# A two-layer graph network on one core: exchanged operands in the degree products, and 16-bit three-part rows in the first layer's gathered sums

## The chip, the cores and the metric

One core of a Trainium2 chip runs the whole program. The metric is device time in microseconds (us) of one execution. TensorE (PE) multiplies matrices and has a separate record for each weight load (PEld); VectorE (DVE), ScalarE (ACT) and GpSimd (POOL) work on tiles; SyncE (SP) issues the plain DMAs and POOL the gathers.

## The reference, cut to what matters

There are 12,500 nodes of 32 features and 212,500 edges sorted by destination. The first layer sums, for every destination, the source rows weighted by the degrees of both ends, adds x and normalises. The second layer computes messages with a small network per edge, sums them the same way and normalises again.

```python
deg = segment_sum(ones, col)
deg_inv_sqrt = where(deg > 0, rsqrt(maximum(deg, 1.0)), 0.0)
norm = deg_inv_sqrt[row] * deg_inv_sqrt[col]
out = segment_sum(x[row] * norm[:, None], col)
x = layernorm(x + out)
x = layernorm(x + L1(x, edge_index, edge_attr_4, edge_attr_32, W1, b1, W2, b2, si_w0, si_w1))
```

## The kernel before, in words

Edges lie in tiles of 128 (one edge per partition), 16 tiles to a chunk. 1664 tiles are needed. An output node's sum is made by TensorE: gathered source rows are the weights of a matmul and a one-hot matrix of the destinations is the moving operand, so the sums land transposed in PSUM and DVE adds them into `sumT_all`, whose columns are nodes.

**Setup.** DVE builds one-hot matrices and TensorE counts the degrees with products (line 721): for each of 11 offsets (`TWIN`) DVE writes a weighted one-hot `ahi` (two operations, lines 1089 and 1092, two buffers in turn) and TensorE runs 16 products. There the shifted one-hot `lox` (128 contiguous 16-bit columns) is the weight and `a[0:CHUNKS, :, t]` (98 columns, each 16 elements from the next) is the moving operand. After the loop DVE remaps gather indices (lines 1114 and 1116; POOL finishes them, 546 and 548), makes the keys of the counted tiles (lines 1118 to 1130), and then, once the degrees are there, the inverse roots and the scaled table of x (lines 1131 to 1146). SP writes that table to memory (463); POOL waits for it and gathers.

**First layer.** It treats its tiles in two ways at once. 880 tiles go through 80 units of 11 tiles: DVE makes two one-hots for a tile (`spread_tile`, 1322 and 1324), TensorE makes a 128-partition count of source rows from them in three products (`count_tile`, 813) into one of two PSUM rings, ACT (10 of 11 tiles, line 619) or DVE (one, line 1331) copies the counts to SBUF, and one unit later TensorE multiplies the counts with the table in SBUF (`apply_counts`, 828: 98 products of 96 columns for a unit). The table holds each scaled row as three 16-bit parts (high, middle, low: ACT lines 605 and 609, DVE lines 1312 and 1316), so its sums have 96 rows and the parts are joined later by a product with `parts` (line 800).

The other 784 tiles are 49 chunks that are gathered. POOL issues 16 indirect DMAs for a chunk (line 551), each fetching 128 rows of 32 fp32 numbers (128 B) from the scaled table, into one of two buffers `xg`. DVE writes the fp32 one-hots of a chunk (`one_hots`, 1190), TensorE makes the sums (`window_sums`, 753: 16 fp32 products of 32 weight and 76 moving columns, each recorded as two), and DVE adds them (`add_gathered`, 1367).

The order is written out by hand. `turn(u)` fixes on TensorE, for every unit, where the sums of a chunk stand (after the count of tile 7 in the units that `chunk_turn` names, 49 of the 80), and POOL may start a quarter of a chunk only when TensorE has reached a pacing point (`s_pace`) and the buffer is free (`s_sum`). The engines run their lists in order: while TensorE waits for a chunk's rows, the units wait too.

**Second layer.** It starts when the first is normalised: POOL gathers normalised rows from `x1_table`, DVE forms products and reductions for each edge (lines 1498, 1504 and 1514). All values take the branch `all_near == 1`; the other branch (`wide_sums`, `add_wide_sums`) doesn't run.

Of the kernel before, what the change touches and what calls it, by code (L numbers as in the profile page):

```python
# [9 lines left out]
I32 = mybir.dt.int32  # L10
# [41 lines left out]
def gnn_program(nc, x_d, src_d, dst_d, first_d, efT_d, sh_d, w1_d, b1_d, w2_d, si_d, out_d):  # L52
# [96 lines left out]
    with ctx:  # L149
# [8 lines left out]
        x1_d = nc.dram_tensor("x1_table", (NPAD, D), F32).ap()  # L158

# [58 lines left out]
        xg = [sb(f"xg{k}", [P, TPC, D]) for k in range(2)]  # L218
# [4 lines left out]
        oh_all = [sb(f"oh{k}", [P, TPC, SW]) for k in range(2)]  # L223
        oh = [[o[:] for o in oh_all]] * 2
        idx0_block = oh_all[1][:].rearrange("p t w -> p (t w)")[:, 0:CG * TPC].bitcast(I32)
# [27 lines left out]
        high = oh_all[0][:].rearrange("p t w -> p (t w)")[:, 0:DT]  # L253
# [5 lines left out]
        ident_b = sb("ident_b", [P, P], BF16)  # L259
# [9 lines left out]
        tile_at = z_row[0:U].rearrange("p g f -> p (g f)")[:, 2 * P + 32:2 * P + 32 + UT]  # L269
        unit_rise = z_sq[:].rearrange("p g f -> p (g f)")[:, 3 * P - 32:3 * P - 32 + U]  # L270
        blocks = q_sb[:, 0:NP, :]
        picked = flat1[:, 0:HB * D].rearrange("p (h f) -> p h f", f=D)
        part_rows = flat1[:, 512:512 + HBS * D].rearrange("p (j f) -> p j f", f=D)
# [18 lines left out]
        ps_sum = [ps[0:m, 7 - l, 0:SPC * SW].rearrange("p (s w) -> p s w", s=SPC) for l, m in enumerate((D, DM))]  # L292
        ps_rows = [ps[:, 7, 0:GB * D]] * 2
# [7 lines left out]
        ps_deg = ps[:, 7, 0:NP]  # L301
        ps_count = ps[0:CHUNKS, 6, 0:TPC * TWIN]
# [19 lines left out]
        s_degree = sem("s_degree")  # L322
        s_root = sem("s_root")
# [3 lines left out]
        s_own = sem("s_own")  # L327
        s_remap = sem("s_remap")
# [82 lines left out]
        def _(sp):  # L411
# [59 lines left out]

            for k in range(2):
                sp.wait_ge(s_g[k], 16 * TPC * ((CG + 1 - k) // 2))
# [29 lines left out]
        def _(pool):  # L503
# [193 lines left out]
        def _(pe):  # L697
# [157 lines left out]
            def pick_rows(tile):  # L855
                pe.wait_ge(s_ohs, tile * 2 + 3)
                pe.matmul(ps_low, ohlow[:, 0, 0:P], ident_b[:], start=True, stop=True).then_inc(s_turned, 1)
# [13 lines left out]
            with pe.Else():  # L871
# [15 lines left out]
                with pe.Fori(1, CG // 2) as i:  # L887
                    for k in range(2):
                        wide_sums(0, xg[k], 2 * i + k, (s_g[k], 16 * TPC * i + 16 * TPC))
                wide_sums(0, xg[0], CG - 1, (s_g[0], 16 * TPC * (CG // 2) + 16 * TPC))  # L890
# [89 lines left out]
        def _(dve):  # L980
# [79 lines left out]
            with dve.If(all_near == 1):  # L1060
# [23 lines left out]
                for i in range(TWIN):  # L1084
                    if i >= 2:
# [8 lines left out]
                                      ALU.mult).then_inc(s_ndoh, 1)  # L1094
            with dve.Else():
# [22 lines left out]
            dve.memset(var[:], 1.0).then_inc(s_key, 1)  # L1118
            dve.wait_ge(s_src, 16 * SRC_LOADS)
            dve.tensor_scalar(low[:].bitcast(I32), dsrc, P - 1, None, ALU.bitwise_and).then_inc(s_key, 1)  # L1120
            dve.tensor_scalar(key[:].bitcast(I32), dsrc, 7, None, ALU.logical_shift_right).then_inc(s_key, 1)
            dve.wait_ge(s_key, 2)
            dve.tensor_copy(low[:], low[:].bitcast(I32)).then_inc(s_key, 1)
            dve.wait_ge(s_key, 3)
            dve.tensor_copy(high, key[:].bitcast(I32)).then_inc(s_key, 1)
            dve.wait_ge(s_key, 5)
            for to, of, offset in zip(counted_places(key), counted_places(high), counted_tiles(rel_tile)):
                dve.scalar_tensor_tensor(out=to, in0=of, scalar=float(TWIN), in1=offset, op0=ALU.mult,
                                         op1=ALU.add).then_inc(s_key, 1)

# [17 lines left out]
            dve.memset(eps[:], EPS).then_inc(s_w2x, 1)  # L1148

# [34 lines left out]
            def one_hots(layer, n):  # L1184
# [5 lines left out]
                dve.tensor_tensor(oh[layer][k], rel_b[:, a:a + TPC].unsqueeze(2).to_broadcast([P, TPC, SW]),  # L1190
# [171 lines left out]
            def add_gathered(n, bases):  # L1362
                dve.wait_ge(s_sum[0], n + 1)
                for v in range(SPC):
                    wait_adds()
                    at = bass.ds(bases[v], SW)
                    dve.tensor_tensor(sumT_all[0:D, at], sumT_all[0:D, at], ps_sum[0][:, v, :],
                                      ALU.add).then_inc(s_acc[0], 1)
                    gathered_adds[0] += 1

            def clear_pads(k):
                dve.memset(counts[k][:, :, UT * TWIN:P], 0.0).then_inc(s_pads, 1)

# [28 lines left out]
            with dve.If(all_near == 1):  # L1402
                for u in range(U + 2):
                    for t in range(UT):
# [8 lines left out]
                        if u == 0 and t == 4:  # L1413
                            one_hots(0, 0)
                            dve.wait_ge(s_remap, 4)
# [26 lines left out]
            with dve.Else():  # L1442
# [3 lines left out]
                dve.tensor_copy(ident_b[:], ident[:]).then_inc(s_ohs, 1)  # L1446
# [9 lines left out]
                for c in range(CPP):  # L1456
                    add_wide_sums(0, c, of=(dst_f, c * TPC))
                with dve.Fori(1, CG // CPP) as i:
                    for c in range(CPP):
                        add_wide_sums(0, i * CPP + c, of=(dst_f, i * PT + c * TPC))  # L1460
                for n in range(CG // CPP * CPP, CG):
# [183 lines left out]
```

## Time and profile before

| | us |
|---|---|
| Median of 3 runs (3302.31 to 3311.62) | 3307.98 |
| The profiled execution | 3305.82 |
| Its span, first to last instruction | 3304.0 |
| First layer, first gather to last sums | 82.6 to 1177.3 |
| Second layer, to the end | about 1192 to 3304 |

The three stages are told apart by gather lines: POOL's gathers with `scaled_x_table` are the first layer's, those with `x_table` the second's. A matmul's record is longer than the distance to the next one, so distances between starts are the rate.

### The profile page before, as it was taken

What the parts mean: (1) busy time and instruction counts of PE and PEld (TensorE: products, weight loads), DVE (VectorE), ACT (ScalarE), POOL (GpSimd) and SP (SyncE); (2) the same over time, 40 slices, a digit from 0 to 9 for tenths busy, and PEclk for the clock granted to TensorE, in tenths of its full rate; (3) what the DMA queues carried; (4) which work ended last, traced back from release to release, by engine and by line L of the source; (5) the groups of instructions that cost most, each with busy time, mean ns of one, the idle gap of its engine ahead of it and who ended that gap; (6) DMA issues with size and microseconds to landing.
All of it is one profiled execution on the core that took longest, in us unless ns stands there. A gap on an engine that the chain in (4) does not pass through costs nothing.

```text
span 3304.0 us, 49643 instructions
## 1 busy us (share of the span) xinstructions
PE 2608.2 (79%) x17448; PEld 1564.6 (47%) x17534; DVE 2882.3 (87%) x5078; ACT 1267.8 (38%) x1963; POOL 2386.6 (72%) x2477
## 2 busy tenths in 40 slices
PE   5799999999989967777777777777777777777776
PEld 4567676766667743333333333333343333333333
DVE  7777877777777749999999999999999999999998
ACT  2787878887878741111111111111111111111111
POOL 1777777777767747777777777777777777777775
PEclk6899999999999988998888989988888888988897
DMA  3000000000000021111111111111111111111112
GB/s 79 13 14 14 14 14 14 14 13 14 14 13 14 14 35 32 28 28 28 28 28 28 28 32 29 28 28 28 28 28 29 31 28 29 28 28 28 28 32 37
DMA packets 169352, 84.63 MB, mean 26 GB/s; under 512 B 112473, under 2 KB 155289, under 8 KB 169113
## 3 DMA queue, kind: packets, MB, share of 16 engines
q0 software_dynamic: 78336, 40.26, 8.2%
q1 hardware_dynamic: 90777, 41.20, 5.3%
q8 instruction: 147, 2.41, 0.3%
q14 instruction: 92, 0.75, 0.1%
HBM read 76.48 MB, written 4.81 MB: 25 GB/s over the span
## 4 chain that ended last, share of the span: by engine, by line
POOL 31%; PE 22%; DVE 22%; issue 14%; ACT 10%; DMA 1%; DVEq 1%; POOLq 0%; SPq 0%; ACTq 0%
POOL xg L551 31%; PE ps L813 10%; ACT room L619 9%; DVE stage L1514 7%; PE ps L828 5%; DVE prod_all L1504 4%; PE ps L753 3%; DVE prod_all L1498 3%; DVE oh L1190 1%; DVE prod_all L1324 1%; DVE stage L1488 1%; PE ps L800 1%; DVE stage L1484 1%; PE ps L721 1%; DVE lane L1322 1%
## 5 line engine op out<-in xcount | busy, mean ns | idle before, releaser
L551 POOL DMA_INDIRECT xg<-x_table,idx x1664 | 1572.6, 945 | 545.4 <-issue 501.6
L551 POOL DMA_INDIRECT xg<-scaled_x_table,efT_all x784 | 801.4, 1022 | 285.7 <-issue 226.0
L619 ACT ACTIVATE room<-ps 128x1089 bf16<-128x1089 f32 x800 | 880.3, 1205 | 204.9 <-PE ps L813 204.5
L936 PE MATMUL ps<-w2t,hT 128*128 128x512 f32 x1664 | 883.7, 657 | 18.1 <-ACT hT L670 17.9
L1514 DVE TENSOR_REDUCE stage<-prod_all 128x192 f32<-128x1536 f32 x416 | 725.4, 1744 | 3.2
L813 PE MATMUL ps<-prod_all,lane 128*128 128x363 bf16 x2640 | 560.8, 321 | 111.1 <-ACT room L619 64.4
L936 PEld LDWEIGHTS ps<-w2t,hT 128*128 128x128 f32 x1664 | 346.7, 214 | 377.3 <-issue 248.0
L828 PE MATMUL ps<-stage,room 128*128 128x96 bf16 x7840 | 465.6, 207 | 0.0
L670 ACT ACTIVATE hT<-ps,b 128x512 f32<-128x512 f32 x208 | 142.9, 687 | 830.1 <-PE ps L924 830.0
L924 PE MATMUL ps<-efT_all,w 128*128 128x512 f32 x416 | 266.5, 727 | 244.6 <-DMA sh<-in_sh 244.2
L828 PEld LDWEIGHTS ps<-stage,room 128*128 128x128 bf16 x7840 | 418.5, 98 | 84.4 <-issue 1.7
L1324 DVE TENSOR_SCALAR prod_all<-near_lanes,key 128x1092 bf16<-128x1092 f16 x880 | 448.7, 510 | 0.0
L678 ACT ACTIVATE stage<-xg 128x64 f32<-128x64 f32 x416 | 105.0, 252 | 889.7 <-DMA xg<-x_table,idx 889.5
L1498 DVE TENSOR_TENSOR prod_all<-ps,stage 128x768 f32<-128x768 f32 x416 | 398.1, 957 | 44.8 <-PE ps L936 26.9
L931 PE MATMUL ps<-b2p,ones_b 128*128 128x512 bf16 x746 | 269.4, 438 | 175.2 <-DVE prod_all L1504 168.2
L1504 DVE TENSOR_TENSOR prod_all<-ps,stage 128x768 f32<-128x768 f32 x416 | 393.5, 946 | 0.0
L1322 DVE TENSOR_SCALAR lane<-low_lanes,low 128x129 bf16<-128x129 f16 x880 | 246.5, 280 | 136.1 <-PE ps L813 132.1
L766 PEld LDWEIGHTS ps<-oh,stage 128*128 128x128 f32 x1664 | 238.4, 191 | 199.3 <-DVE stage L1523 124.7
L766 PE MATMUL ps<-oh,stage 128*128 128x152 f32 x1664 | 256.6, 298 | 84.3 <-DVE stage L1523 84.3
L813 PEld LDWEIGHTS ps<-prod_all,lane 128*128 128x128 bf16 x2640 | 203.3, 98 | 241.5 <-DVE prod_all L1324 115.5
L931 PEld LDWEIGHTS ps<-b2p,ones_b 128*128 128x128 bf16 x832 | 75.7, 106 | 430.6 <-DVE prod_all L1504 297.4
L924 PEld LDWEIGHTS ps<-efT_all,w 128*128 128x128 f32 x416 | 80.6, 216 | 310.0 <-DMA sh<-in_sh 258.6
(155 smaller groups left out, 1627.5 us busy)
## 6 DMA issues: line engine op xcount, KB each, us to landing
efT_all<-in_efT SPq DMA_DIRECT2D x104, 256.0 KB
xg<-x_table,idx POOLq DMA_INDIRECT x1664, 2.4
xg<-scaled_x_table,efT_all POOLq DMA_INDIRECT x784
sh<-in_sh SPq DMA_DIRECT2D x104, 32.0 KB
idx<-in_src SPq DMA_DIRECT2D x104, 8.0 KB, 1.6
scaled_x_table<-room SPq DMA_DIRECT2D x2, 784.0 KB, 3.4
x_table<-x_sb SPq DMA_DIRECT2D x7, 224.0 KB, 4.4
out_rows<-room SPq DMA_DIRECT2D x6, 224.0 KB
```

What stands on the lines that cost most here:

```text
L551: pool.indirect_dma_start(to, None, table, bass.IndirectOffsetOnAxis(ap=at, axis=0)).then_inc(landed, 16)
L619: act.activation(counts[u % 2][:, :, t * TWIN:(t + 1) * TWIN].rearrange("p (r h) w -> p r h w", r=RANGES), ps_ring[i % 2].rearrange("p r ( ...
L766: mm = pe.matmul(ps_pair, msg[k][:, SPC * t:SPC * (t + 1), :].rearrange("p s f -> p (s f)"), oh[1][k][:, t::TPS, :], start=(t == 0), stop= ...
L813: mm = pe.matmul(ps_ring[i % 2][:, r, :], ohlow[:, i % LR, 0:P], spread[i % KR][:, r * RW:(r + 1) * RW], start=True, stop=True)
L828: mm = pe.matmul(ps_dense, counts[u % 2][:, h, :], table[:, h, :], start=(h == 0), stop=(h == NP - 1))
L924: pe.matmul(ps_h2, w1[:, 2 * m:2 * m + 2, :].rearrange("p g h -> p (g h)"), efT[k], start=True, stop=True).then_inc(s_h, 1)
L931: pe.matmul(ps_bank[j % 2][v], ones_b[:], b2p[:].rearrange("p h f -> p (h f)"), start=True, stop=False)
L936: mm = pe.matmul(ps_bank[j % 2][v], hT[j // 2][:, t * P:(t + 1) * P], w2t[:].rearrange("p h c o i -> p (h c o i)"), start=False, stop=True)
L1324: dve.tensor_scalar(spread[i % KR], near_lanes[:], key[:, i:i + 1], None, ALU.is_equal).then_inc(s_spread, 1)
L1498: dve.tensor_tensor(prod[b][:, :, 0:3], ps_w[b][:, :, 0:3 * MUL * MUL].rearrange("p t (c o i) -> p t c o i", c=3, o=MUL), feat[k][:, cut]. ...
L1504: dve.tensor_tensor(prod[b][:, :, 3:6], ps_w[b][:, :, 3 * MUL * MUL:].rearrange("p t (o i) -> p t o i", o=MUL).unsqueeze(2) .to_broadcast( ...
L1514: dve.tensor_reduce(msg[k][:, TPG * j:TPG * (j + 1), 2 * MUL:DM], prod[j % 2].rearrange("p t c o i -> p t (c o) i"), AX_X, ALU.add).then_i ...
```

## The change

1. In the degree products weights and moving operand are exchanged: the strided one-hot (98 columns) is loaded as weights and the 128 contiguous columns of `lox` move. The counts come out transposed, are copied by DVE to `degT` and turned back by one fp32 product with the identity.
2. DVE's degree chain and scaled table are moved ahead of the keys of the counted tiles.
3. SP writes the three-part table from SBUF to memory as rows of 96 16-bit numbers (192 B) once its low part is made.
4. From the third chunk on POOL gathers such rows, the one-hots are 16-bit, and the sums are 16-bit products with 96 weight columns; DVE adds 96 rows.
5. Buffers of gathered rows and one-hots share one tensor, so that the wider rows fit; the branch that doesn't run is adapted (`join_parts`).

```diff
+        split_d = nc.dram_tensor("split_table", (NPAD, D3), BF16).ap()
...
+            sp.wait_ge(s_low_part, 1)
+            sp.dma_start(split_d.rearrange("(l h) f -> l h f", l=P), table).then_inc(s_split, 16)
...
                 if n >= 2:
                     pool.wait_ge(s_sum[0], n - 1)
+                    pool.wait_ge(s_split, 16)
...
-                    gather_rows(xg[n % 2][:, t, :], y_d, idx0[:, n * TPC + t:n * TPC + t + 1], s_g[n % 2])
+                    gather_rows((xg if n < 2 else xs)[n % 2][:, t, :], y_d if n < 2 else split_d, idx0[:, n * TPC + t:n * TPC + t + 1], s_g[n % 2])
...
-                        mm = pe.matmul(ps_deg, lox[:, t, TWIN - 1 - i:LX - i], a[0:CHUNKS, :, t], start=False, stop=False)
+                        mm = pe.matmul(ps_degT, a[0:CHUNKS, :, t], lox[:, t, TWIN - 1 - i:LX - i],
+                                       start=(i == 0 and t == 0), stop=(i == TWIN - 1 and t == TPC - 1))
                     mm.then_inc(s_ndmm, 1)
+                pe.wait_ge(s_degT, 1)
+                pe.matmul(ps_deg, degT, ident[0:NP, 0:NP], start=False, stop=False)
...
+                to, rows, ones = (ps_sum[0], xg[k], oh[0][k]) if n < 2 else (ps_sum3, xs[k], oh_b[k])
                 for t in range(TPC):
-                    mm = pe.matmul(ps_sum[0][:, t // TPS, :], xg[k][:, t, :], oh[0][k][:, t, :],
+                    mm = pe.matmul(to[:, t // TPS, :], rows[:, t, :], ones[:, t, :],
...
+                dve.wait_ge(s_ndmm, TWIN)
+                dve.tensor_copy(degT, ps_degT).then_inc(s_degT, 1)
...
+            dve.wait_ge(s_degree, 1)
+            step(dve.tensor_copy(deg[:], ps_deg))
+            dve.tensor_scalar(root[:], deg[:], 1.0, None, ALU.max).then_inc(s_maxdeg, 1)
...
             dve.memset(var[:], 1.0).then_inc(s_key, 1)
...
-            dve.wait_ge(s_degree, 1)
-            step(dve.tensor_copy(deg[:], ps_deg))
-            dve.tensor_scalar(root[:], deg[:], 1.0, None, ALU.max).then_inc(s_maxdeg, 1)
...
-                dve.tensor_tensor(oh[layer][k], rel_b[:, a:a + TPC].unsqueeze(2).to_broadcast([P, TPC, SW]),
+                dve.tensor_tensor(oh_b[k] if layer == 0 and n >= 2 else oh[layer][k], rel_b[:, a:a + TPC].unsqueeze(2).to_broadcast([P, TPC, SW]),
...
+                    rows, of = (D, ps_sum[0]) if n < 2 else (D3, ps_sum3)
+                    dve.tensor_tensor(sumT_all[0:rows, at], sumT_all[0:rows, at], of[:, v, :],
```

## Rows read from the trace of the kernel before

**Rows 1.** Stages: length, busy PE, PEld, DVE, ACT, POOL, clock, DMA share, GB/s.
```profile
76.00:1192.00 1116.00, 995.76 (x12404) 760.69 (x12404) 850.84 (x2230) 887.99 (x890) 801.45 (x784) 0.98 0.10 17
1192.00:3304.00 2112.00, 1567.00 (x4761) 769.43 (x4847) 1974.83 (x2755) 359.50 (x1062) 1572.60 (x1664) 0.89 0.15 29
```
**Rows 2.** The chain that ended last: sums of three chunks in a row, and the last.
```profile
206.10 2.23 PE ps L753 x32
...
220.09 2.22 PE ps L753 x32
...
245.82 2.22 PE ps L753 x32
...
1175.05 2.22 PE ps L753 x32
```
**Rows 3.** PE and ACT in order of time behind one chunk's sums.
```profile
222.25 0.60 PE L828 MATMUL ps<-stage,room 128*128 128x96 bf16 x10
222.68 0.63 PE L813 MATMUL ps<-prod_all,lane 128*128 128x363 bf16 x3
...
223.35 3.43 ACT L619 ACTIVATE room<-ps 128x1089 bf16<-128x1089 f32 x3 [2.14 <-PE ps L813]
```
**Rows 4.** POOL by line, and its waits for PE (us, times, longest), 76 to 1192 us.
```profile
L551 POOL DMA_INDIRECT xg<-scaled_x_table,efT_all x784 | 801.4, 1022 | 285.7 <-issue 226.0 <-PE ps L828 33.9 <-PE ps L753 14.9
POOL xg L551 <- PE ps L828: 33.9, 65, 5.6
POOL xg L551 <- PE ps L753: 14.9, 10, 7.7
```
**Rows 5.** POOL and DVE in order of time: first gather, low part, a slow gather, last gather.
```profile
82.60 3.77 POOL L551 DMA_INDIRECT xg<-scaled_x_table,efT_all  x1 [10.84 <-DMA scaled_x_table<-room]
...
89.60 3.42 DVE L1316 TENSOR_TENSOR stage<-room,stage 128x3136 bf16<-128x3136 f32 x1
...
225.94 1.40 DVE L1190 TENSOR_TENSOR oh<-rel_b,near_lanes 128x1216 f32<-128x1216 bf16 x1
226.06 2.11 POOL L551 DMA_INDIRECT xg<-scaled_x_table,efT_all  x1 [0.30 <-issue]
...
1157.99 0.95 POOL L551 DMA_INDIRECT xg<-scaled_x_table,efT_all  x1 [0.30 <-issue]
```
**Rows 6.** Chain, 28 products of 128 fp32 weight and 32 moving columns.
```profile
322.17 3.05 PE ps L800 x28
```
**Rows 7.** Setup products of line 707, 25.3 to 26 us: ns min, median, max.
```profile
L707 PE MATMUL ps<-room,ones_at x12: 239/239/239, 25.1 to 26.0; 128*104 128x176 bf16 x12
L707 PEld LDWEIGHTS ps<-room,ones_at x11: 127/127/128, 25.2 to 26.0; 128*104 128x104 bf16 x11
```
**Rows 8.** The chain: landing of a table's half, of the first chunk's last rows.
```profile
78.21 3.47 DMA scaled_x_table<-room
...
109.93 2.47 DMA xg<-scaled_x_table,efT_all
```
**Rows 9.** DVE by line, 200 to 1100 us: busy, mean ns, idle before.
```profile
L1190 DVE TENSOR_TENSOR oh<-rel_b,near_lanes 128x1216 f32<-128x1216 bf16 x41 | 58.0, 1414 | 0.0
```
**Rows 10.** Setup in order of time, PE and DVE.
```profile
37.65 10.70 PE L721 MATMUL ps<-room 104*128 104x98 bf16 x59 [6.47 <-DVE room L1092]
...
60.72 0.98 DVE L1089 TENSOR_TENSOR room<-prod_all,lane 104x1568 bf16<-104x1568 bf16 x1 [0.87 <-PE ps L721]
...
63.58 0.97 DVE L1089 TENSOR_TENSOR room<-prod_all,lane 104x1568 bf16<-104x1568 bf16 x1 [0.88 <-PE ps L721]
...
69.08 0.26 PE L730 MATMUL ps<-zero_b 128*128 128x98 bf16 x1
70.11 2.65 DVE L1128 SCALAR_TENSOR_TENSOR key<-oh,room 128x792 f32<-128x792 f32 x2
72.68 0.24 DVE L1132 COPY deg<-ps 128x98 f32<-128x98 f32 x1
```
**Rows 11.** A stretch of the degree products, columns as in Rows 1.
```profile
48.00:54.00 6.00, 6.00 (x35) 4.30 (x34) 4.18 (x5) 0.00 (x0) 0.00 (x0) 0.50 0.00 0
```

More of the change, by code:

```diff
@@ L217, in gnn_program @@
         idx = [sb(f"idx{k}", [P, TPC], I32) for k in range(2)]
-        xg = [sb(f"xg{k}", [P, TPC, D]) for k in range(2)]
+        SPLIT = TPC * D3 // 2
+        OH_AT = SPLIT + TPC * D
+        gathered = sb("gathered", [P, OH_AT + 2 * TPC * SW])
+        xg = [gathered[:, k * SPLIT:k * SPLIT + TPC * D].rearrange("p (t f) -> p t f", f=D) for k in range(2)]
+        xs = [gathered[:, k * SPLIT:(k + 1) * SPLIT].bitcast(BF16).rearrange("p (t f) -> p t f", f=D3) for k in range(2)]
         sh = [sb(f"sh{k}", [P, TPC, 4]) for k in range(2)]
@@ L222, in gnn_program @@
         idx0 = efT_all[:].rearrange("p k e -> p (k e)")[:, 0:CG * TPC].bitcast(I32)
-        oh_all = [sb(f"oh{k}", [P, TPC, SW]) for k in range(2)]
+        oh_all = [gathered[:, OH_AT + k * TPC * SW:OH_AT + (k + 1) * TPC * SW].rearrange("p (t w) -> p t w", w=SW)
+                  for k in range(2)]
+        oh_b = [gathered[:, at:at + TPC * SW // 2].bitcast(BF16).rearrange("p (t w) -> p t w", w=SW)
+                for at in (2 * SPLIT, OH_AT + TPC * SW)]
+        assert 2 * SPLIT + TPC * SW // 2 <= OH_AT + TPC * SW
         oh = [[o[:] for o in oh_all]] * 2
-        idx0_block = oh_all[1][:].rearrange("p t w -> p (t w)")[:, 0:CG * TPC].bitcast(I32)
+        idx0_block = oh_all[0][:].rearrange("p t w -> p (t w)")[:, 0:CG * TPC].bitcast(I32)
         stage = sb("stage", [P, NP * D3 // 2])
@@ L252, in gnn_program @@
         dst_c = key
-        high = oh_all[0][:].rearrange("p t w -> p (t w)")[:, 0:DT]
+        high = oh_all[1][:].rearrange("p t w -> p (t w)")[:, 0:DT]
         unit_first = sb("unit_first", [1, U], I32)
@@ L258, in gnn_program @@
         parts = sb("parts", [P, D])
-        ident_b = sb("ident_b", [P, P], BF16)
+        ident_b = lane_i[:, 0:P // 2].bitcast(BF16)
         flat = prod_all[:].rearrange("p b t c i o -> p (b t c i o)")
@@ L301, in gnn_program @@
         ps_deg = ps[:, 7, 0:NP]
+        ps_degT = ps[0:NP, 5, 0:P]
         ps_count = ps[0:CHUNKS, 6, 0:TPC * TWIN]
@@ L322, in gnn_program @@
         s_degree = sem("s_degree")
+        s_degT = sem("s_degT")
         s_root = sem("s_root")
@@ L327, in gnn_program @@
         s_own = sem("s_own")
+        s_split = sem("s_split")
+        s_whole = sem("s_whole")
         s_remap = sem("s_remap")
@@ L856, in pick_rows @@
                 pe.wait_ge(s_ohs, tile * 2 + 3)
-                pe.matmul(ps_low, ohlow[:, 0, 0:P], ident_b[:], start=True, stop=True).then_inc(s_turned, 1)
+                pe.matmul(ps_low, ohlow[:, 0, 0:P], ident_b, start=True, stop=True).then_inc(s_turned, 1)
                 pe.wait_ge(s_turnedc, tile + 1)
@@ L886, in _ @@
                     wide_sums(0, xg[k], k, (s_g[k], 16 * TPC))
[L887 to L890, printed above, removed]
+                with pe.Fori(2, CG) as n:
+                    wide_sums(0, whole_rows, n, (s_whole, 2 * n - 2))
                 with pe.Fori(0, DT // TPC) as m:
@@ L1116, in _ @@
             dve.tensor_scalar(idx0, idx0, P - 1, None, ALU.bitwise_and).then_inc(s_remap, 1)
[L1118 to L1129, printed above, removed]
             dve.wait_ge(s_degree, 1)
@@ L1148, in _ @@
             dve.memset(eps[:], EPS).then_inc(s_w2x, 1)
+            dve.memset(var[:], 1.0).then_inc(s_key, 1)
+            dve.wait_ge(s_src, 16 * SRC_LOADS)
+            dve.tensor_scalar(low[:].bitcast(I32), dsrc, P - 1, None, ALU.bitwise_and).then_inc(s_key, 1)
+            dve.tensor_scalar(key[:].bitcast(I32), dsrc, 7, None, ALU.logical_shift_right).then_inc(s_key, 1)
+            dve.wait_ge(s_key, 2)
+            dve.tensor_copy(low[:], low[:].bitcast(I32)).then_inc(s_key, 1)
+            dve.wait_ge(s_key, 3)
+            dve.tensor_copy(high, key[:].bitcast(I32)).then_inc(s_key, 1)
+            dve.wait_ge(s_key, 5)
+            for to, of, offset in zip(counted_places(key), counted_places(high), counted_tiles(rel_tile)):
+                dve.scalar_tensor_tensor(out=to, in0=of, scalar=float(TWIN), in1=offset, op0=ALU.mult,
+                                         op1=ALU.add).then_inc(s_key, 1)
             def prepare_weights():
@@ L1372, in clear_pads, with join_parts @@
                 dve.memset(counts[k][:, :, UT * TWIN:P], 0.0).then_inc(s_pads, 1)
+            def join_parts(n):
+                k = n % 2
+                dve.wait_ge(s_g[k], 16 * TPC * (n // 2 + 1))
+                dve.wait_ge(s_sum[0], n)
+                dve.tensor_tensor(whole_rows, xs[k][:, :, 2 * D:D3], xs[k][:, :, D:2 * D], ALU.add).then_inc(s_whole, 1)
+                dve.wait_ge(s_whole, 2 * n - 3)
+                dve.tensor_tensor(whole_rows, whole_rows, xs[k][:, :, 0:D], ALU.add).then_inc(s_whole, 1)
             def add_picked_rows(m, t):
@@ L1445, in _ @@
                 low_part()
-                dve.tensor_copy(ident_b[:], ident[:]).then_inc(s_ohs, 1)
+                dve.tensor_copy(ident_b, ident[:]).then_inc(s_ohs, 1)
                 dve.wait_ge(s_ohs, 1)
@@ L1455, in _ @@
                 dve.wait_ge(s_far, 3)
[L1456 to L1461, printed above, removed]
+                for n in range(CG):
+                    if n >= 2:
+                        join_parts(n)
                     add_wide_sums(0, n, of=(dst_f, chunk_tile(n)))
```

6 lines of the change are left out of this document (4 added, 2 removed).

## The prediction, made before the result was known

> **What bounds it now.** I read the page's slices first, then the stages. The second layer is 2112 us with DVE busy 1975 [rows 1]; the change leaves its instructions alone, so it is carried over unchanged. The first layer is 1116 us, with PE busy 996 at a granted clock of 0.98. A busy share doesn't say what a chunk's sums cost, so the chain comes next. Sums of consecutive chunks start 13.99 us apart when they fall in neighbouring units (206.10 to 220.09) and 25.73 with one unit between (220.09 to 245.82) [rows 2]. So a unit with sums takes 13.99 and one without 25.73 − 13.99 = 11.74: the difference, 2.25, is the sums' own 2.23. PE makes no counts in them, and ACT, which copies the counts, idles 2.14 us in front of its next piece [rows 3]. What leaves the sums therefore comes off the unit, until another engine holds it.
>
> That engine is near: POOL. Its 784 gathers are busy 801.4 us [rows 4], and from the first start, 82.60, to the last end, 1157.99 + 0.95 = 1158.94, are 1076.3 us [rows 5]. The usual gap between two gathers is 0.30 (the bracket of the slow one there); 783 of them are 235. So only 1076.3 − 801.4 − 235 = 40 us are anything more. Waits put down to PE are 33.9 + 14.9 = 48.8 in 65 + 10 gaps [rows 4]; less 75 × 0.30 they are 26 us. The other 14 are issue, and stay. A faster PE can take 26 us from POOL's stretch and no more.
>
> **Chunk sums on PE, 47 chunks.** Removed: 32 records in 2.23 us, 70 ns apart. Added: 16 products with 96 weight and 76 moving 16-bit columns. Ten products of line 828 (128 weight, 96 moving columns) take 222.68 − 222.25 = 0.43 us [rows 3], 43 ns each: 96 columns at 2.4 GHz are 40. Line 800 has 128 fp32 weight columns and 32 moving ones: 3.05 / 28 = 109 ns [rows 6], so there the load sets the rate and the product hides beside it. Which holds for 96 16-bit weight columns? Line 707 loads 104 such columns in records of 127 ns, its products being 239 [rows 7]; that is the nearest type, and far below line 800's long fp32 loads. Line 828's 43 is the lower bound, line 800's 109 the upper. I take 43: 16 × 0.043 = 0.69 us, 1.54 saved, × 47 = 72 us on PE's side (at 109: 1.74, and 23).
>
> The Trainium skill (TensorE: Matmul & The Clock Gate, LDWEIGHTS) puts a load at columns / 1.2 ns: 80 ns for 96 columns, and so 1.3 us for the sums, an estimate. By it PE's side would save 43 us, still about what POOL's side below allows; line 707's 127 ns, with any fixed part inside, neither proves nor excludes it.
>
> **Gathers on POOL.** 752 of them, from the third chunk on, fetch 192 B rows in place of 128 B, and the trace has no 192 B gather. Lower bound: nothing, as each still fetches 128 rows, and 0.95 is the undisturbed record [rows 5]. Upper: all of it grows with the bytes, 0.95 to 1.42, 752 × 0.47 = 353 us. I take nothing: DMA engines are 0.10 busy [rows 1], and a landing of 2.47 us [rows 8] lies outside POOL's record.
>
> The new wait for the written table stands ahead of the third chunk, and behind it queue all further gathers. The low part ended at 89.60 + 3.42 = 93.0 [rows 5]; a table's half of 0.8 MB took 3.47 us [rows 8], so 2.4 MB some 10. At 103 (a few us either way, with the setup's shift) it is written, while POOL needs 32 gathers of over 1.25 for its first two chunks and gets to the wait beyond 114. If that cover fails, a late table costs its lateness once. On SP the write stands ahead only of waits for the gathers' end.
>
> If POOL sets the end of the first layer, four terms move it. (a) Its waits for PE: 26. (b) The slack behind it: the last sums start at 1175.05 [rows 2], 16.1 us after the last gather, and need 2.5 for the landing [rows 8], so 13.6 go, and 1.5 as these sums are shorter: 15. (c) DVE's one-hot of a chunk, 1.41 us [rows 9], holds gathers up: one that starts inside it lasts 2.11 and not 0.95 [rows 5]; in the 77 gathers that touch one, the excess over 0.94 adds up to 32 us. Written in 16 bits it stays at 1.41, or halves as setup's 16-bit operation does (1568 elements in 0.98 us [rows 10], so 0.76 for 1216). The excess shrinks like the length or faster: 0 to 20 us saved. I take 8, below the middle, since one operand repeats each element, unlike in that row. (d) Setup:
>
> **Degree products and DVE's order.** The products stand 178 ns apart ((10.70 − 0.36) / 58 [rows 10]) at a granted clock of 0.50, the 1.2 GHz level [rows 11]. 98 columns are 82 ns there, so the strided moving operand costs twice its columns. An offset takes 63.58 − 60.72 = 2.86 us = 16 × 178, and DVE waits 0.88 in it [rows 10]. Exchanged, 128 contiguous columns move, 107 ns at that level. The strided 98 become weights: 82 ns if a load reads them at full rate, 178 if it pays what the moving operand paid; no row shows a strided load. I take the former, nearer to line 828, whose loads never show: an offset is then 1.71 on PE, and DVE binds with two operations, 1.95. Ten offsets × 0.9 are 9 us, and PE's last batch is 1.15 shorter: 10 in all. The counts' copy, fp32 product and waits are some 0.9 us (0.24 and 0.26 for neighbouring small steps [rows 10]) and lie beside DVE's two index operations of 1.1.
>
> The degree chain started at 72.68, behind the keys, though PE had ended at 69.3 [rows 10]. Now it starts at about 60.5: 69.0 − 10, copy 0.3, index operations 1.2. From 72.68 to the first gather, 82.60, are 9.9, so gathers begin at 70.4, 12.2 earlier. The keys' last pair, 2.65, then lies beside the first gather, as other two-input operations did (record 3.77 [rows 5]), and takes up to 1.9 back: (d) is 10. The keys' six us follow the chain, so units start 6 us earlier, too.
>
> **The sum.** POOL's side: 26 + 15 + 8 + 10 = 59, less 5, an estimate, for waits that remain where both sides are close: 54. PE's side: 72 + 6 = 78, so it is ahead by some 20 and does not end last. The profiled execution took 3305.8 (span 3304.0): 3305.8 − 54 = 3251.8. It lies 2.2 under the median, so 3254. Late next is POOL, from the third chunk to the last, with PE waiting for rows. DVE's adds over 96 rows have the columns of those over 32, and cost nothing more.
>
> **Rivals.** *The exchange gives nothing*: a strided load at 178 ns. PE still ends at 69, gathers start at 80.2, 2.4 earlier, less 1.9, and units 3.6 later: (d) is 0.5, the sum 44, time 3263. For it: the same 98 strided elements are read for each product. Against: elsewhere loads stay beside products.
>
> The Trainium skill (SBUF — State Buffer, SBUF: two separate sides) says that accesses within one 16-byte line run at full bandwidth and each new line is penalised. By that rule this rival holds, every element being 32 B from the next; the moving operand's 178 ns agree with it, for loads no row here does.
>
> *Wider rows cost POOL time* (slower). Place: each of 752 gathers; POOL has no room, so each ns counts 0.75 us. It decides from 54 / 0.752 = 72 ns on, 8% of 0.95. If half of the record goes with the bytes, each is 0.235 longer: 177 − 54 = +123, time 3431. For it: no row of that width. Against: each still asks for 128 rows.
>
> *POOL's waits come back*: PE, stopped in order at a chunk's sums, reaches the pacing points late, so that (a) and (b) stay and (c) and (d), 18 or less, are all: 3290 to 3308. Against: the waits for PE are short today (5.6 and 7.7 at most [rows 4]) although PE is the slower one.
>
> **How the numbers follow.** Forecast 0.52; exchange without gain 0.29; waits that come back 0.11, half of it within 0.3% of before; wider rows 0.08. The range goes from 3234 (no remaining waits, c at 20: 71, and a few more) to 3286 (no exchange, c at 0, remaining waits 10: 31, and 10 ns for each gather, 8). 0.3%, 10 us, is about what a measurement of this kernel can tell. Faster 0.86, same 0.06, slower 0.08.
>
> **What would show it.** Right: sums of a chunk near 0.7 us on PE; PE waiting for rows, and POOL hardly for PE; undisturbed gathers at 0.95; the first gather near 70; an offset near 1.95. Wrong: gathers above 1.02, a POOL that still waits for PE by tens of us, or a first gather at 80.

## The result, and the profile after

| | before | after |
|---|---|---|
| Median of 6 runs each, us | 3310.41 | 3287.01 |
| Lowest and highest, us | 3302.31, 3314.51 | 3280.84, 3291.27 |
| Ratio, 95% interval | | 0.9936 [0.9923, 0.9948] |
| The profiled execution, its span, us | 3305.82, 3304.0 | 3286.16, 3284.4 |

The change makes the kernel 0.64% faster, 21 us; the forecast was 54. The sign held, and POOL came onto the path, though for about half of it only. Of the four terms of the forecast the waits came as forecast, the slack came to two thirds, the setup to nothing, and the one-hots turned into a loss. In the profiled pair the span is 19.6 us shorter, and the working below adds up to that.

The stages of the kernel after (length; busy PE, PEld, DVE, ACT, POOL; clock; DMA share; GB/s), against [rows 1]:
```profile
76.00:1172.00 1096.00, 938.76 (x11652) 711.61 (x11652) 852.32 (x2237) 889.05 (x890) 812.79 (x784) 0.95 0.15 25
1172.00:3284.40 2112.40, 1567.26 (x4847) 766.37 (x4847) 1975.23 (x2755) 355.38 (x1062) 1573.10 (x1664) 0.90 0.15 29
```
The second layer is the same length to 0.4 us; the whole gain lies in the first. There PE is busy 57 us less and POOL 11.3 more.

The chain that ended last of the kernel after: the last rows that it waits for, the last two chunks' sums and what follows them (start, duration, what), against [rows 2]:
```profile
1039.47 2.43 DMA gathered<-split_table,efT_all
...
1134.00 0.71 PE ps L777 x16
...
1153.83 0.71 PE ps L777 x16
1154.54 1.71 PE ps L852 x40
...
1156.54 3.47 issue
...
1161.13 6.17 PE ps L824 x28
```
Sums of a chunk take 0.71 us in place of 2.22. The last of them start 21.2 us earlier than before. In what follows them about 3 us go back: the engines stand 3.47 us in the "issue" behind line 648, and the 28 joins take 6.17. In the kernel before the same two pieces took 1.25 and 5.56, and the gap from the last sums' end to the second layer's first gather was 18.7 us; now it is 21.7.

POOL of the kernel after by line (busy, mean ns, idle before and releasers), and the waits that changed (us, times, longest), against [rows 4]:
```profile
L570 POOL DMA_INDIRECT gathered<-split_table,efT_all x752 | 773.4, 1028 | 240.4 <-issue 229.1 <-PE ps L852 10.7 <-PE ps L777 0.6
L570 POOL DMA_INDIRECT gathered<-scaled_x_table,efT_all x32 | 39.4, 1231 | 17.3 <-issue 8.5 <-DMA scaled_x_table<-room 7.8 <-PE ps L852 0.6
POOL gathered L570 <- PE ps L852: 11.3, 37, 0.3
PE ps L777 <- DMA gathered<-split_table,efT_all: 34.1, 11, 7.1
```
The waits have changed sides. POOL's waits for PE are 0.3 us at most, which is the usual gap between two gathers; PE now waits 34.1 us, in 11 pieces, for a chunk's rows.

How far POOL sets the first layer is told by the chain, from the first sums to the last; its shares, before (112.4 to 1175.05 us) and after (113.8 to 1153.83):
```profile
by line: PE ps L813 30.4%; ACT room L619 28.0%; PE ps L828 16.8%; PE ps L753 9.9%; DVE prod_all L1324 3.3%; issue 2.8%; DVE lane L1322 2.1%; PE ps L800 1.8%; PE ps L839 1.2%; POOL xg L551 1.1%; DVE room L1331 0.6%; DMA xg<-scaled_x_table,ef
by line: POOL gathered L570 33.1%; PE ps L837 16.2%; ACT room L639 14.7%; issue 14.3%; PE ps L852 9.4%; PE ps L777 2.4%; DVE prod_all L1347 2.1%; DMA gathered<-split_table,efT_all 1.9%; PE ps L824 1.5%; DVE lane L1345 1.3%; PE ps L863 0.7%;
```
Gathers were 1.1% of it and are 33.1%, beside 14.3% of "issue", in which the gaps between gathers lie. The other half is still the units, on PE and ACT. The two take turns, and the last turn is the units': rows landed at 1039.47 + 2.43 = 1041.90 are the last that the chain waits for, 112 us ahead of the last sums.

The same stretches by engine (columns as in [rows 1]); then two chunks' sums in order of time, one behind a wait for rows and the last one; then the few us behind that wait, by engine again:
```profile
112.40:1175.05 1062.65, 967.77 (x12188) 742.89 (x12189) 811.15 (x2146) 862.59 (x868) 776.80 (x767) 0.99 0.10 16
113.80:1153.83 1040.03, 911.24 (x11456) 694.45 (x11456) 809.85 (x2150) 864.91 (x870) 787.85 (x766) 0.97 0.14 21
1041.94 1.50 PE L777 MATMUL ps<-gathered 128*96 128x76 bf16 x16 [4.67 <-DMA gathered<-split_table,efT_all]
1153.67 0.88 PE L777 MATMUL ps<-gathered 128*96 128x76 bf16 x16
1041.00:1046.00 5.00, 4.06 (x40) 3.50 (x41) 1.16 (x4) 0.81 (x1) 3.78 (x5) 0.50 0.13 20
```
The stretch is 22.6 us shorter: PE is busy 56.5 us less and waits 30.9 us more for rows (3.2 before, 34.1 now); 3 us are other gaps. The 47 changed sums alone save 47 × 1.51 = 71 us, so some 14 us came back elsewhere on PE. The granted clock fits that: its mean went from 0.99 to 0.97, and behind the wait of 4.67 us that ends at 1041.94 it is 0.50, the 1.2 GHz level, where the same sums take 1.50 us and not 0.88. That all of the 14 us are the clock is not shown.

POOL and DVE of the kernel after in order of time (start, duration, instruction): the first gather, a one-hot with the gather that starts inside it, the last gather; against [rows 5]:
```profile
83.40 1.29 POOL L570 DMA_INDIRECT gathered<-scaled_x_table,efT_all  x1 [7.82 <-DMA scaled_x_table<-room]
...
249.52 1.41 DVE L1213 TENSOR_TENSOR gathered<-rel_b,near_lanes 128x1216 bf16<-128x1216 bf16 x1
249.63 2.11 POOL L570 DMA_INDIRECT gathered<-split_table,efT_all  x1 [0.30 <-issue]
...
1145.11 0.94 POOL L570 DMA_INDIRECT gathered<-split_table,efT_all  x1 [0.30 <-issue]
```
POOL's stretch in numbers: first gather at 83.40 (+0.8), records 812.8 us (+11.3), gaps between them 1146.05 − 83.40 − 812.8 = 249.9 (−25.0). So the last gather ends 12.9 us earlier, at 1146.05. The last sums start 7.8 us behind it, no longer 16.1: another 8.3. Together 21.2.

A line's busy time in the same kernel, 200 to 1100 us, against [rows 9]:
```profile
L1213 DVE TENSOR_TENSOR gathered<-rel_b,near_lanes 128x1216 bf16<-128x1216 bf16 x41 | 57.9, 1411 | 0.0
```
The one-hot written in 16 bits takes 1411 ns, as the fp32 one did (1414).

The degree products of the kernel after, all 176, and DVE in their loop and behind it, against [rows 10]:
```profile
L741 PEld LDWEIGHTS ps<-room x176: 259/280/283, 37.4 to 69.4; 104*98 104x98 bf16 x176
```
```profile
61.15 0.97 DVE L1111 TENSOR_TENSOR room<-prod_all,lane 104x1568 bf16<-104x1568 bf16 x1 [0.95 <-PE ps L741]
...
64.08 0.98 DVE L1111 TENSOR_TENSOR room<-prod_all,lane 104x1568 bf16<-104x1568 bf16 x1 [0.95 <-PE ps L741]
...
69.94 0.29 DVE L1118 COPY z_sq<-ps 98x128 f32<-98x128 f32 x1 [3.87 <-PE ps L741]
...
71.26 0.25 DVE L1143 COPY deg<-ps 128x98 f32<-128x98 f32 x1
71.54 0.83 DVE L1144 TENSOR_SCALAR root<-deg 128x98 f32<-128x98 f32 x1
...
73.89 5.05 DVE L1153 TENSOR_TENSOR room<-x_sb,dinv 128x1568 f32<-128x1568 f32 x2
```
An offset takes 64.08 − 61.15 = 2.93 us (before 2.86), and DVE still waits 0.95 in each. The strided load's record is 280 ns long; before, the load of 128 contiguous columns was 127. The degree chain starts at 71.26, only 1.4 earlier than before, and its scaled table takes 5.05 us.

### The profile page after: what moved, and what is told of

The parts are those of the page before. It is cut to its first block, busy times and chain, and to the rows that moved or that the text cites. A ratio compares the mean times of both kernels' runs of the same rounds, so it can differ in the third digit from the quotient of the medians.

```text
span 3284.4 us, 48231 instructions
## 1 busy us (share of the span) xinstructions
PE 2552.5 (78%) x16784; PEld 1521.8 (46%) x16784; DVE 2879.5 (88%) x5079; ACT 1264.7 (39%) x1963; POOL 2397.6 (73%) x2477
## 4 chain that ended last, share of the span: by engine, by line
POOL 34%; DVE 30%; issue 16%; PE 12%; ACT 5%; DMA 1%; DVEq 1%; POOLq 0%; SPq 0%; ACTq 0%
POOL gathered L570 34%; DVE stage L1543 10%; DVE prod_all L1533 5%; PE ps L837 5%; ACT room L639 5%; DVE prod_all L1527 4%; PE ps L852 3%; DVE gathered L1213 2%; DVE stage L1517 2%; DVE stage L1513 1%; PE ps L741 1%; DVE stage L1552 1%; PE ps L824 1%; PE ps L777 1%; DVE prod_all L1347 1%
## 5 line engine op out<-in xcount | busy, mean ns | idle before, releaser
L570 POOL DMA_INDIRECT gathered<-x_table,idx x1664 | 1573.1, 945 | 538.6 <-issue 502.0
L570 POOL DMA_INDIRECT gathered<-split_table,efT_all x752 | 773.4, 1028 | 240.4 <-issue 229.1
L958 PE MATMUL ps<-w2t,hT 128*128 128x512 f32 x1664 | 875.4, 652 | 19.6 <-ACT hT L690 19.5
L837 PE MATMUL ps<-prod_all,lane 128*128 128x363 bf16 x2640 | 569.1, 325 | 116.1 <-ACT room L639 62.4
L852 PE MATMUL ps<-stage,room 128*128 128x96 bf16 x7840 | 473.4, 209 | 0.0
L852 PEld LDWEIGHTS ps<-stage,room 128*128 128x128 bf16 x7840 | 427.7, 99 | 81.9 <-issue 4.2
L953 PE MATMUL ps<-b2p,ones_b 128*128 128x512 bf16 x832 | 288.5, 433 | 186.8 <-DVE prod_all L1533 186.2
L698 ACT ACTIVATE stage<-gathered 128x64 f32<-128x64 f32 x416 | 104.7, 252 | 792.8 <-DMA gathered<-x_table,idx 792.6
L790 PEld LDWEIGHTS ps<-gathered,stage 128*128 128x128 f32 x1664 | 239.7, 193 | 215.4 <-DVE stage L1552 143.0
L790 PE MATMUL ps<-gathered,stage 128*128 128x152 f32 x1664 | 259.1, 300 | 98.5 <-DVE stage L1552 98.5
```

The costliest lines, as they stand in the source:

```text
L570: pool.indirect_dma_start(to, None, table, bass.IndirectOffsetOnAxis(ap=at, axis=0)).then_inc(landed, 16)
L790: mm = pe.matmul(ps_pair, msg[k][:, SPC * t:SPC * (t + 1), :].rearrange("p s f -> p (s f)"), oh[1][k][:, t::TPS, :], start=(t == 0), stop= ...
L837: mm = pe.matmul(ps_ring[i % 2][:, r, :], ohlow[:, i % LR, 0:P], spread[i % KR][:, r * RW:(r + 1) * RW], start=True, stop=True)
L852: mm = pe.matmul(ps_dense, counts[u % 2][:, h, :], table[:, h, :], start=(h == 0), stop=(h == NP - 1))
L953: pe.matmul(ps_bank[j % 2][v], ones_b[:], b2p[:].rearrange("p h f -> p (h f)"), start=True, stop=False)
L958: mm = pe.matmul(ps_bank[j % 2][v], hT[j // 2][:, t * P:(t + 1) * P], w2t[:].rearrange("p h c o i -> p (h c o i)"), start=False, stop=True)
```

## Experiments

Ratios are to the kernel before on the same chip, with 95% intervals. "Excess" is the sum, over the gathers that touch a chunk's one-hot in time, of their record's length over the usual 0.945, worked out from POOL's and DVE's records in order of time; "records" is the sum over the first layer's 784 gathers.

| run | ratio | records | excess | last gather starts |
|---|---|---|---|---|
| the kernel before | 1 | 801.4 | 32 | 1157.99 |
| the kernel after | 0.9936 [0.9923, 0.9948] | 812.8 | 43 | 1145.11 |
| e1_setup_only | 1.0006 [0.9997, 1.0015] | 802.6 | 31 | 1158.97 |
| e2_rows_only | 0.9931 [0.9918, 0.9944] | 812.4 | 44 | 1141.82 |
| e3_after_lanes_psum | 0.9860 [0.9845, 0.9874] | 787.4 | 10 | 1118.25 |
| e4_before_lanes_psum | 0.9987 [0.9979, 0.9996] | 775.5 | 4 | 1151.21 |
| e5_after_contig_weights | 0.9904 [0.9890, 0.9918] | 811.2 | 42 | 1131.63 |
| e6_after_half_onehots | 0.9866 [0.9850, 0.9882] | 795.8 | 28 | 1126.55 |
| e7_lanes_old_operands_early_indices | 0.9858 [0.9843, 0.9873] | 786.7 | 11 | 1113.72 |
| e8_before_contig_moving | 0.9970 [0.9958, 0.9982] | 803.6 | 33 | 1150.17 |
| e9_half_lanes | 0.9849 [0.9831, 0.9867] | 789.4 | 16 | 1117.77 |
| e10_half_onehots_old_operands | 0.9882 [0.9865, 0.9899] | 794.2 | 26 | 1121.93 |
| e11_onehots_late | 0.9926 [0.9912, 0.9940] | 814.3 | 43 | 1146.78 |
| e12_onehots_early | 0.9936 [0.9923, 0.9950] | 817.3 | 42 | 1150.17 |

### The two halves of the change, each alone (e1, e2)

e1 puts part 1 and 2 of the change (exchange, order of DVE's setup) into the kernel before; e2 takes them back out of the kernel after (of its edit, the operands):

```diff
-                        mm = pe.matmul(ps_degT, a[0:CHUNKS, :, t], lox[:, t, TWIN - 1 - i:LX - i],
-                                       start=(i == 0 and t == 0), stop=(i == TWIN - 1 and t == TPC - 1))
+                        mm = pe.matmul(ps_deg, lox[:, t, TWIN - 1 - i:LX - i], a[0:CHUNKS, :, t], start=False, stop=False)
...
-                pe.wait_ge(s_degT, 1)
-                pe.matmul(ps_deg, degT, ident[0:NP, 0:NP], start=False, stop=False)
```


> The kernel before with the setup half of the change alone (exchanged degree products, degree chain ahead of the keys; fp32 rows as before). Theory: a strided load costs what the strided moving operand cost, about 183 ns a product, so the degree loop ends about 1 us later and gathers start at 83 to 84 (82.6 before), units some 4 us later; PE binds the first layer here, so the time is 0 to 5 us longer than before. Rival (the exchange helps, and its gain is lost later in the changed kernel): first gather at 75 or earlier, time 3 to 10 us shorter.

> The changed kernel with the old setup (old operands, keys ahead of the degree chain): only the 16-bit rows and sums are left. Theory: the rows carry the whole gain, since POOL starts at 82.6 and its records bind: 18 to 24 us under before, within 4 us of the changed kernel. Rival (the new setup gives something, the rows little): less than 12 us under before. Second rival (the setup takes back what the rows give): over 28 us under before.

The setup half alone changes nothing that can be measured, and its first gather starts at 83.60, as its theory had it. The rows alone bring all of it, 0.9931. So one term of the forecast, (d), is zero, and the others have to be looked for in the gathered rows.

### What the exchange runs into: the stride (e5, e8)

Both read the strided operand from contiguous elements instead, 98 in a row; e5 as the exchanged kernel's weights, e8 as the old kernel's moving operand. These elements are not the one-hot's, so neither kernel computes the true degrees.

```diff
-                        mm = pe.matmul(ps_degT, a[0:CHUNKS, :, t], lox[:, t, TWIN - 1 - i:LX - i],
+                        mm = pe.matmul(ps_degT, ohhi[0:CHUNKS, 2048 * (i % 2) + NP * t:2048 * (i % 2) + NP * (t + 1)], lox[:, t, TWIN - 1 - i:LX - i],
```


> The changed kernel with the 98 weight columns of the degree products read from neighbouring places (the degrees computed are then not the reference's). Theory (the stride sets the load's 183 ns): products 107 ns apart, DVE's two operations bind an offset at 1.95 us, the loop ends 10 us earlier, and as POOL binds the first layer, nearly all of it reaches the end: first gather at 73 to 75, time 7 to 11 us under the changed kernel. Rival (the stride is not the reason: short loads of fewer than 128 columns, or the clock): offsets stay at 2.9 us and the time within 2 us of the changed kernel.

> The kernel before with the 98 moving columns of the degree products read from neighbouring places (the degrees computed are then not the reference's). Theory: without the stride the products are 82 to 107 ns apart and DVE binds an offset at 1.95 us, the loop ends 10 us earlier; the keys then stand in front of the degree chain, so gathers start some 8 us earlier, and the units too, so 6 to 10 us less than before. Rival: 178 ns are the products' rate at this size whatever the stride: no difference.

The degree products of e5, the weight loads and a batch of 16 (start, duration):
```profile
L741 PEld LDWEIGHTS ps<-room x176: 120/203/208, 37.5 to 58.7; 104*98 104x98 bf16 x176
```
```profile
57.20 1.94 PE L741 MATMUL ps<-room 104*98 104x128 bf16 x16 [0.18 <-DVE room L1114]
```
And a batch of e8:
```profile
56.10 1.49 PE L721 MATMUL ps<-room 104*128 104x98 bf16 x16 [0.40 <-DVE room L1092]
```
Without the stride the products of e5 stand (1.94 − 0.31) / 15 = 109 ns apart, and the 128 moving columns are 107 at the 1.2 GHz level (the granted clock is 0.50 there, as in [rows 11]); those of e8 (1.49 − 0.28) / 15 = 81, with 98 columns at 82. With the stride it was 183 and 178, whichever side it lay on. In e5 PE waits for DVE, the loop ends at 59.1, the first gather starts at 72.63, and the end comes 0.9936 − 0.9904 = 0.0032, some 10.6 us, earlier (the two intervals, of 0.0014 to either side, do not meet). That is (d) as it was forecast, had the load run at full rate: 10. In e8 the first gather starts at 73.08, and the time is 0.9970 of before, some 10 us less: the old order gains as much from contiguous elements.

The rival in the prediction took a rule of the Trainium skill (SBUF — State Buffer, SBUF: two separate sides), the penalty for each access that crosses to a new 16-byte line, to hold for weight loads too. That section speaks of accesses in general; the runs agree for loads, with 183 ns against 109.

### What the gathers run into: the one-hots (e3, e4, e6, e11, e12)

e3 copies the row of lanes once to PSUM, so that a chunk's one-hot reads only one operand from SBUF, and writes it two tiles later in the unit. e4 is the same edit in the kernel before.

```diff
+            dve.tensor_copy(ps_lanes, near_lanes[:].bitcast(F32)[:, 0:SW // 2]).then_inc(s_lanes, 1)
...
-                spans_of = near_lanes[:, 0:SW] if layer == 0 else ps_mlane
+                spans_of = (near_lanes[:, 0:SW] if n < 2 else ps_lanes.bitcast(F16)) if layer == 0 else ps_mlane
...
-            def add_unit(u):
+            def add_unit(u, then):
...
+                for n in then:
+                    one_hots(0, n)
...
-                        if t == 4 and u >= 1:
-                            for n in chunks_of(u - 1):
-                                if n + 2 < CG:
-                                    one_hots(0, n + 2)
...
-                            add_unit(u - 2)
+                            add_unit(u - 2, [n + 2 for n in chunks_of(u - 1) if n + 2 < CG])
```


> The changed kernel; from the third chunk on the one-hots read the lane numbers from PSUM (16-bit, packed, written once in setup) and not from SBUF, and stand two tiles later in DVE's order, ahead of the unit's add. Theory (POOL's records bind, and 43 us of them are gathers held up beside a one-hot that reads two tiles from SBUF): that excess falls under 8 us, the gathers end some 35 us earlier, and the 34 us that PE waits for rows shrink to under 10, so the time is 22 to 36 us under the changed kernel, 3250 to 3266. Rival (PE waits because 192 B rows land late or pacing is late, not because POOL is full): within 5 us of the changed kernel.

> The kernel before with the same edit of the one-hots. Theory: PE binds its first layer, so POOL's records shrink by some 30 us and its waits for PE grow by as much: time within 5 us of before. Rival (POOL's records bound the kernel before as well): 20 us or more under before.

e3, DVE and POOL in order of time around a one-hot, to be held against the pair at 249.5 above:
```profile
313.14 1.42 DVE L1217 TENSOR_TENSOR gathered<-rel_b,ps 128x1216 bf16<-128x1216 bf16 x1
313.25 0.94 POOL L572 DMA_INDIRECT gathered<-split_table,efT_all  x1 [0.30 <-issue]
```
The one-hot is as long as ever, and a gather that starts 0.11 us inside it, as in the other pair, is not held: 0.94 in place of 2.11. The records shrink by 25.4 us, the last gather starts 26.9 earlier, and the end follows with 0.9936 − 0.9860, some 25 us. The time is the expected one; the sizes behind it are smaller than expected (an excess of 10 and not under 8, 26.9 us and not 35, and 16 us of waits for rows left, not under 10). In e4 the records shrink by as much, 25.9, and the ratio is 0.9987, some 4 us. There most of POOL's saved time turns into waits for PE:
```profile
L553 POOL DMA_INDIRECT xg<-scaled_x_table,efT_all x784 | 775.5, 989 | 305.3 <-issue 228.0 <-PE ps L830 38.7 <-PE ps L755 27.8
```
38.7 + 27.8 us, where the kernel before had 33.9 + 14.9 [rows 4]: 17.7 more. One edit, worth 25 us in one kernel and 4 in the other: that shows that the rows put POOL's records on the path, where PE's had stood alone.

e3 changed the place of the one-hot too. e11 keeps that place and has both operands in SBUF; e12 writes the one-hots at tile 2 in place of 4 (`if t == 2 and u >= 1:`).

> The changed kernel with the chunk's one-hots at the later place that the run with the lanes in PSUM gave them (inside the addition of a unit, at tile 6 in place of tile 4), but with both operands in SBUF. If the operand's home is what that run gained by: a gather that touches a one-hot still costs 0.4 to 0.7 us more (43.4 / 71 = 0.61 in the changed kernel), gathers of 2.1 us are there, the excess is 25 to 60 us, and the time lies within 12 us of 3287. If the later place was the gain: excess of at most 15 us, no gather of 2.1, time near 3262.

> The changed kernel with the chunk's one-hots at tile 2 in place of tile 4, nothing else. If the rise of the gathers' records (32 us of excess before, 43 after) comes from where the one-hots fall against the gathers: the count of 2.1 us gathers moves away from 24 by 6 or more, to either side, the excess with it (by 8 us or more), and the time by about the same number of us. If the 16-bit writing itself makes a collision dearer: count, excess (43 within 5) and time (3287 within 6) stay.

The place is worth nothing: excess 43 and 42, ratios 0.9926 and 0.9936. So e3's gain is the operand's home. The first theory of e12 missed: 21 gathers last over 2.0 us, no longer 25, but the excess and the time stayed. In e11 only 7 are over 2.0, 25 others last 1.8, and the sum is the same again.

Whether a 16-bit one-hot makes each meeting dearer, e12's second theory, whose signs came, the traces of the two kernels settle. Gathers of the third chunk on, by how long after a one-hot's start they start (count, mean us):

| | 0.05 to 0.4 us | 0.4 to 0.7 | 0.7 to 1.0 | 1.0 to 1.35 |
|---|---|---|---|---|
| before, fp32 one-hots | 15, 2.11 | 7, 1.68 | 2, 1.47 | 21, 1.03 |
| after, 16-bit one-hots | 24, 2.11 | 8, 1.66 | 11, 1.43 | 4, 1.03 |

At the same place the price is the same. In both kernels each of these gathers ends 0.81 to 0.82 us after the one-hot. What rose is the number that start in the first 1.0 us, from 24 to 43 (e1 24, e2 44). So the rise from 32 to 43 us comes from where POOL's gathers and DVE's one-hots meet, not from the writing; why they meet there more often, no run shows.

e6 leaves both operands in SBUF and writes a chunk's one-hot in two halves, at tiles 4 and 7:

```diff
-                                    one_hots(0, n + 2)
+                                    half_one_hots(n + 2, 0)
+                        if t == 7 and u >= 1:
+                            for n in chunks_of(u - 1):
+                                if n + 2 < CG:
+                                    half_one_hots(n + 2, 1)
```


> The changed kernel with each chunk's one-hots made in two operations of half the tiles, three tiles apart in DVE's order; both still read two tiles from SBUF. Theory (a gather that starts inside such an operation waits for its end, so the excess goes as the square of its length): 43 us of excess become 18 to 27, the time is 10 to 22 us under the changed kernel. Rival (every operation costs a gather a fixed amount, whatever its length): excess stays or doubles, time the same or longer.

A half takes 779 ns; the excess falls from 43 to 28 us, records by 17, the last gather starts 18.6 earlier, and the ratio goes to 0.9866, some 23 us less, both just outside what was expected (18 to 27 and 10 to 22). DVE does more work for it (98 × 0.78 = 76 us, no longer 49 × 1.41 = 69) and the kernel is faster.

The rule of the Trainium skill (SBUF — State Buffer, Who interferes with whom) is that a DVE operation with at most one SBUF input, outside the modes in which it uses two ports, keeps out of GpSimd's way, and one with two stands in the way of a GpSimd instruction that reads SBUF. The pair 2.11 and 0.94 agrees with it, if a gather, whose row numbers lie in SBUF, is such an instruction.

### Towards a faster kernel (e7, e9, e10)

e7 is e3 with the old operand order and DVE's two index operations inside the degree loop, so that POOL finishes its indices before the scaled table is made. e9 adds e6's halves, in two neighbouring units; e10 is e6 with e7's setup.

```diff
+                    if i == 6:
+                        split_indices()
```


> The version put together from the parts: 16-bit rows, lane numbers in PSUM, the old operands of the degree products, the degree chain ahead of the keys, and the two index operations inside the degree loop, where DVE waits for PE. Theory: degrees are there at 69, and the scaled table's operations no longer share the time with POOL's index operations (5.05 us beside them, 3.49 without), so gathers start at 78 to 80; POOL and PE are close to each other by now, so 1 to 5 us of it reach the end: 3254 to 3261. Rival (the table's slow operations have another cause): first gather at 82 or later, the time that of the version with lanes in PSUM alone, or longer.

> The version put together from the parts (16-bit rows, lane numbers in PSUM, old operands, index operations in the degree loop), with each chunk's one-hots in two halves, made in two neighbouring units. In the version with whole one-hots PE waits 65 us for DVE's one-hots of tiles, since 1.41 us of DVE in one piece stand ahead of them. Theory (POOL and PE by now bind together): half the piece takes some 30 us of these waits away; POOL's stretch stays, so 3 to 12 us under that version: 3250 to 3259. Rival (POOL alone binds): within 2 us of it.

> The changed kernel with one-hots in two halves from SBUF, and with the old operands and the index operations in the degree loop. Theory: gathers start near 79.9 and not 83.6; POOL binds, so 3 us of these 3.7 reach the end: 3262 to 3265. Rival: the time of the halves alone, 3266, or longer.

In e7 the first gather starts at 79.88 and the table's operations are back at 3.49 us, but its 0.9858 is not told apart from e3's 0.9860; e9's 0.9849 is not told apart from either, where 3 to 12 us less were expected, and e10 is no better than e6. e9 is the lowest ratio of all: 1.5% under the kernel before, 0.9% under the kernel after. Gathers are 12.3, 20.9 and 13.8% of the chains of e3, e7 and e9 from the first sums to the last, where they were 33.1 in the kernel after, and the larger part is PE and ACT again; which to shorten first stays open. The waits of e3 that are left on PE's side (us, times, longest):
```profile
PE ps L839 <- DVE prod_all L1351: 77.1, 102, 10.8
PE ps L839 <- ACT room L641: 31.4, 68, 5.6
PE ps L779 <- DMA gathered<-split_table,efT_all: 16.0, 6, 4.9
```
PE still waits 16 us for rows, but 77 for DVE's one-hots of the counted tiles (43.7 in the kernel after); what of the two is worth more there, no run separates.

## Why the prediction was right, and where it failed

Steps (c) and (d) failed, with 18 us forecast and a loss of 12.1 measured, and step (b) in part.

**The bound.** Right in the main. POOL comes onto the path, PE waits for rows, and e3 beside e4 shows it by what the same edit is worth. But "from the third chunk to the last" is too much: about half of the chain is POOL's, and its last 112 us in front of the last sums are the units'.

**PE's side**, 72 + 6 forecast, "ahead by some 20", so that it "does not end last": it was less far ahead. The sums saved their 71 us, but some 14 came back on PE, at a lower mean clock, for which the forecast had no term; and the units did not start 6 us earlier but 4 later (first count at 83.40, before at 79.39), as (d) failed.

**Sums of a chunk**, 0.69 forecast: 0.71. Line 828's rate was the right row; the load of 96 16-bit columns hides. At 44 ns for each product the 1.3 us that stand beside it as an estimate are out.

**Width of rows** at nothing: right. Gathers that touch no one-hot have a median of 0.944 us in both kernels. The wider-rows rival is out. The table is written in 7.8 us and no gather waits for it: it costs nothing, as argued.

**(a) POOL's waits for PE**, 26: the gaps shrank by 25.0. Right. The waits that come back, the third rival, did not.

**(b) The slack at the end**, 15: 8.3 from the slack and 1.5 from shorter sums, 9.8. The step "so 13.6 go" failed. It took the last rows' landing for the only thing between the last gather and the last sums. But from sums to sums, 1134.00 to 1153.83, PE and ACT have 19.8 us of the units' own work, with no wait for rows in the chain (none since 1041.90), so 7.8 of slack stay and not 2.5. And 3 us of the gain went back behind the sums.

**(c) The one-hots**, 8 less: 11 more. "Written in 16 bits it stays at 1.41, or halves": it stayed, and the forecast took a value between the ends. One operand that repeats each element is not like the setup's row, as was noted there and not followed. Beyond that the lower end, "0", was not the lower end: the excess rose from 32 to 43 us, and where POOL is the bound each of these counts. The runs show the price (e3, e6) and that only the rows bring the rise (e1 31, e2 44). It is not the 16-bit writing, as the price of a meeting stayed: more gathers, 43 and not 24, start in a one-hot's first 1.0 us. That POOL, which no longer pauses for PE, meets the one-hots more often for that reason is likely and not shown; e12 rules out the place in the unit.

**(d) Setup**, 10: nothing, which is the rival "the exchange gives nothing" (e1). "I take the former, nearer to line 828, whose loads never show" failed: the strided load pays the stride as the moving operand did, 183 ns and not 82, and an offset took 2.93 us, not 1.95. Line 828 reads contiguous weights and was the wrong row; the nearest row was the strided operand itself, 178 ns. e5 shows that the rest of the step, 10 us earlier gathers for 10 us of time, was right. Two smaller losses lie in the order: the chain now runs beside POOL's index operations (71.45 to 75.6), and line 1153 takes 5.05 us, where line 1142 of the kernel before took 3.49:
```profile
74.69 3.49 DVE L1142 TENSOR_TENSOR room<-x_sb,dinv 128x1568 f32<-128x1568 f32 x2
```
So even the 2.4 us that the rival left for the first gather went, and it came 0.8 later.

Summed up by POOL's side: 26 + 15 + 8 + 10 − 5 was forecast. Measured are 25.0 + 9.8 − 11.3 − 0.8 = 22.7, less 3 behind the sums: 19.7, against 19.6 of the span. (The forecast's 5 for remaining waits falls away: POOL has none but the usual gaps.)

## What to carry to other kernels

When a change moves the bound to another engine, what this engine shares with its neighbours becomes the price of the whole: look for the records of the new bound that are longer than the usual one, and for what runs beside them. A bound can move for a part of the path only: read the chain by stretches, up to its end, before a saving on one engine is carried to the time. A strided operand sets about the same pace on either side of a matmul here (183 and 178 ns), so exchanging operands does not remove it; laying the operand out contiguously does (e5, e8). And a cost with two ends belongs to the end whose row has the same access pattern, not between them.

## What was not expected of the hardware

- A gather that starts inside a one-hot with both inputs in SBUF ends 0.81 to 0.82 us after it, up to 2.11 in place of 0.94, with fp32 and with 16-bit output alike; with one input in PSUM, at the same length of the operation, it is 0.94, and 1.10 when it starts in the last 0.2 us.
- It goes the other way too: beside POOL's two index operations the scaled table took DVE 5.05 us, 3.49 without them.
- Behind a wait of 4.67 us for rows the granted clock of TensorE was 0.50, and a chunk's sums took 1.50 us in place of 0.88.
- A load of 98 16-bit columns 32 B apart takes 280 ns and leaves 183 between products; contiguous it is 203 and 109 (the kernel after and e5, granted clock 0.50).
- A 192 B row costs POOL no more than one of 128 B.
